# Attention product in three passes, with lists re-ordered, in a two-layer graph kernel

## The reference

```python
# layer 0
q, k = split(X @ Wqk);  v = X @ Wv
agg = einsum('bij,bjd->bid', adj, k * mask)
w = mask * einsum('bid,bid->bi', q, agg) / 16
x = layernorm(x + softmax(w, axis=1)[:, :, None] * v)
# layer 1
query, keyt, value = x @ Wq.T + bq, x @ Wk.T + bk, x @ Wv.T + bv
weight = adj * exp(einsum('bqd,bkd->bqk', query, keyt))
weight = weight / sum(weight, axis=2)
x = layernorm(x + einsum('bqk,bkd->bqd', weight, value))
```

## Time and profile before

| | |
|---|---|
| Median of 3 runs | 305.21 us (304.97 to 305.28) |
| Profiled execution | 305.32 us |
| Its span | 303.5 us |
| TensorE matmul busy | 97% |
| VectorE busy | 75% |
| ScalarE busy | 71% |
| GpSimd busy | 65% |
| Mean granted TensorE clock | 0.994 |
| DMA | 103 GB/s |

### The profile page before, as it was taken

How to read it: one execution, slowest core, us unless ns; L and a number is a source line. 1 busy time by engine, 2 the same in 40 slices (tenths; PEclk the granted TensorE clock), 3 DMA queues, 4 the chain that set the end, 5 groups by cost and what they waited for, 6 DMA issues and landing times.

```text
span 303.5 us, 6829 instructions
## 1 busy us (share of the span) xinstructions
PE 293.9 (97%) x1956; PEld 269.4 (89%) x1956; DVE 227.3 (75%) x691; ACT 215.0 (71%) x509; POOL 198.2 (65%) x237
## 2 busy tenths in 40 slices
PE   8999999999999999999999999999999999999981
PEld 7788999999999999999999999999999999999980
DVE  1476778877777887777788777778877777888583
ACT  3447667778877777887777788777778877776762
POOL 1547766666886666688666667866666787664540
PEclk9999999999999999999999999999999999999997
DMA  7921233332334332224334222434422234210102
GB/s 230 339 73 36 88 89 122 97 107 62 105 121 121 121 113 92 70 89 121 121 121 121 80 73 89 121 121 121 121 89 72 83 119 121 87 54 36 37 35 104
DMA packets 19165, 31.26 MB, mean 103 GB/s; under 512 B 2128, under 2 KB 6608, under 8 KB 19152
## 3 DMA queue, kind: packets, MB, share of 16 engines
q1 hardware_dynamic: 19152, 31.11, 32.6%
HBM read 22.71 MB, written 8.39 MB: 102 GB/s over the span
## 4 chain that ended last, share of the span: by engine, by line
PE 91%; DVE 4%; issue 2%; ACT 1%; POOL 1%; POOLq 0%; DVEq 0%
PE ps L789 22%; PE ps L791 21%; PE ps L790 21%; PE ps L897 8%; PE ps L892 8%; PE ps L874 4%; PE ps L996 1%; PE ps L812 1%; PE ps L849 1%; PE ps L843 1%; DVE stats L571 1%; PE ps L1001 1%; DVE x L609 1%; PE ps L854 1%; POOL x1t_lo_a L303 0%
## 5 line engine op out<-in xcount | busy, mean ns | idle before, releaser
L355 POOL TENSOR_TENSOR rstd<-var_eps,minus_half 128x4 f32<-128x4 f32 x31 | 31.6, 1018 | 72.4 <-DVE var_eps L711 72.4
L431 ACT ACTIVATE x<-x_sum,shift,rstd 128x256 f32<-128x256 f32 x62 | 33.9, 595 | 59.7 <-POOL shift L358 59.6
L789 PE MATMUL ps<-w_hi,xt_hi 128*128 128x512 f32 x128 | 56.8, 444 | 0.5 <-DVE w_lo L775 0.5
L791 PE MATMUL ps<-w_hi,xt_lo 128*128 128x512 f32 x128 | 50.3, 393 | 0.0
L790 PE MATMUL ps<-w_lo,xt_hi 128*128 128x512 f32 x128 | 50.3, 393 | 0.0
L282 POOL TENSOR_TENSOR x1b<-x,bv_all 128x512 f32<-128x512 f32 x32 | 41.3, 1290 | 6.7 <-DVE x L609 3.5
L365 POOL TENSOR_TENSOR xt_lo<-xt_raw,xt_hi 128x512 fp32r<-128x512 f32 x31 | 39.8, 1285 | 3.0 <-ACT xt_hi L413 3.0
L342 POOL TENSOR_TENSOR x_lo<-x_raw,x_hi 128x512 fp32r<-128x512 f32 x28 | 36.1, 1290 | 3.4 <-ACT x_hi L420 2.1
L789 PE MATMUL ps<-wv_hi,x1t_hi 128*128 128x258 f32 x124 | 37.9, 305 | 0.0
L791 PE MATMUL ps<-wv_hi,x1t_lo 128*128 128x258 f32 x124 | 35.3, 285 | 0.0
L790 PE MATMUL ps<-wv_lo,x1t_hi 128*128 128x258 f32 x124 | 35.1, 283 | 0.0
(11 more groups left out here) (128 smaller groups left out, 787.9 us busy)
## 6 DMA issues: line engine op xcount, KB each, us to landing
xt_raw<-xt_pairs SPq DMA_DIRECT2D x32, 256.0 KB, 2.8
x_raw<-x_pairs SPq DMA_DIRECT2D x32, 256.0 KB, 3.1
out_pairs<-x SPq DMA_DIRECT2D x31, 256.0 KB, 2.5
adjt<-adjt_pairs SPq DMA_DIRECT2D x32, 129.0 KB, 2.0
p<-params SPq DMA_DIRECT2D x1, 770.0 KB, 7.1
p<-params SPq DMA_DIRECT2D x1, 512.0 KB, 3.8
p<-params SPq DMA_DIRECT2D x1, 256.0 KB, 4.9
out_pairs<-x SPq DMA_DIRECT2D x2, 128.0 KB, 1.8
```

What stands on the lines that cost most here:

```text
L355: nc.gpsimd.tensor_tensor(rstd[r % 2][:, :, :], var_eps[:, :, :], minus_half[:, :, :], ALU.pow)\
L431: last = nc.scalar.activation(out[:, graph(g)], in_[:, graph(g)], ACT.Identity, bias=shift[r % 2][:, layer, g:g + 1], scale=rstd[r % 2][:, ...
L789: nc.tensor.matmul(out, s_hi, m_hi, start=first, stop=False)
L791: return nc.tensor.matmul(out, s_lo, m_hi, start=False, stop=last)
```

## The change

New tiles `edge_hi`, `edge_lo`, `val_hi`, `val_lo` hold the parts of the edge and of the value, and in the slots the attention product is a `split_product` of these. ScalarE makes edge_hi (a cast) and val_hi (in place of the copy to val), GpSimd makes edge_lo, VectorE makes val_lo from PSUM. In DRAIN and in the drain the product stays as it was.

The lists are re-ordered. TensorE: attend after both halves of project. VectorE: statistics, neg_mean, var_eps and val_lo before x1t_hi and x1t_lo; both weights together before the attention result; statistics of x2 after the maximum of the row. ScalarE: edge_hi after x1t; split_adjm before the z copy. GpSimd: edge_lo first, then rstd and shift, low_x, mask_adj, xt_lo, low_adjm, x1b. In slot 0 the normalization of x1 is done by VectorE, transpose_w stands between the two values, and transpose_p before the transposes of x1. In the drain some steps are cut into halves of the features or into the two graphs and shared between engines.

```diff
@@ GpSimd, drain and slot
-                nc.gpsimd.tensor_tensor(x1t_lo_a[:, :, :, :].rearrange("p t g n -> p (t g n)"),
-                                        x1t_a[:, :, :, :].rearrange("p t g n -> p (t g n)"),
-                                        x1t_hi_a[:, :, :, :].rearrange("p t g n -> p (t g n)").bitcast(F32),
+                nc.gpsimd.tensor_tensor(x1t_lo_a[:, 0, :, :], x1t_a[:, 0, :, :], x1t_hi_a[:, 0, :, :].bitcast(F32),
                                         ALU.subtract).then_inc(x1t_lo_done, 1)
             def slot(t, r):
-                if exists(t + 3) and r + 3 >= SPLIT:
-                    low_x(t + 3, r + 3)
+                if exists(t - 1):
+                    pool.wait_ge(edge_hi_done, t)
+                    nc.gpsimd.tensor_tensor(edge_lo[:, :], edge[:, :], edge_hi[:, :].bitcast(F32), ALU.subtract)\
+                        .then_inc(edge_lo_done, 1)
...
                 if exists(t + 3) and r + 3 >= SPLIT:
+                    low_x(t + 3, r + 3)
                     mask_adj(t + 3, r + 3)
...
+                if exists(t + 3) and r + 3 >= SPLIT:
+                    low_adjm(t + 3, r + 3)
...
-                if exists(t + 3) and r + 3 >= SPLIT:
-                    low_adjm(t + 3, r + 3)
@@ ScalarE, slot
+                if exists(t - 1):
+
+                    act.wait_ge(edge_done, t)
+                    if exists(t - 2):
+                        act.wait_ge(sum_done, t - 1)
+                    nc.scalar.copy(edge_hi[:, :], edge[:, :]).then_inc(edge_hi_done, 1)
...
+                if exists(t + 3) and r + 3 >= SPLIT:
+                    split_adjm(t + 3, r + 3)
                 if exists(t) and r != 0:
                     act.wait_ge(z_done, t + 1)
                     bias_z(z)
...
-                if exists(t + 3) and r + 3 >= SPLIT:
-                    split_adjm(t + 3, r + 3)
...
-                    nc.scalar.copy(val[:, :, 0:DIM], val_ps[:, :, 0:DIM]).then_inc(val_copied, 1)
+                    to = val if r == DRAIN else val_hi
+                    nc.scalar.copy(to[:, :, 0:DIM], val_ps[:, :, 0:DIM]).then_inc(val_copied, 1)
@@ VectorE, slot
-                        dve.wait_ge(sum_done, t - 1)
+                        dve.wait_ge(edge_lo_done, t - 1)
                     nc.vector.tensor_tensor(edge[:, :], exp_s[:, :], adjt[(r - 1) % 4][:, 0:PAIR_N], ALU.mult)\
                         .then_inc(edge_done, 1)
-                if exists(t) and r != 0:
-                    split_x1t(t)
...
+                if exists(t - 1):
+
+                    dve.wait_ge(val_copied, t)
+                    nc.vector.tensor_tensor(val_lo[:, :, 0:DIM], val_ps[:, :, 0:DIM], val_hi[:, :, 0:DIM].bitcast(F32),
+                                            ALU.subtract).then_inc(val_lo_done, 1)
+                if exists(t) and r != 0:
+                    split_x1t(t)
...
-                    weight(t + 2, r + 2, 0)
+                    for g in range(2):
+                        weight(t + 2, r + 2, g)
...
+                if r == 0:
+                    normed_x1(1, 0, norms(0))
+                if exists(t - 1):
+                    dve.wait_ge(x2_done, t)
+                    both_stats(1, x2[(r - 1) % 4]).then_inc(stats2_done, 1)
@@ TensorE, slot
-                if exists(t - 1):
-
-                    pe.wait_ge(edge_done, t)
-                    pe.wait_ge(val_copied, t)
-                    attend(sum_ps, edge, val, 0)
-                    attend(sum_ps, edge, val, 1).then_inc(sum_done, 1)
                 if exists(t + 2):
                     project(t + 2, r + 2, 1)
+                if exists(t - 1):
+
+                    pe.wait_ge(edge_lo_done, t)
+                    pe.wait_ge(val_lo_done, t)
+                    for g in range(2):
+                        n = graph(g, NODES)
+                        mm = split_product(sum_ps[:, g, 0:VAL_COLS], [(edge_hi[:, n], edge_lo[:, n],
+                                                                       val_hi[:, g, :], val_lo[:, g, :])])
+                    mm.then_inc(sum_done, 1)
...
                     values(x1t_hi, x1t_lo, 0)
-                    values(x1t_hi, x1t_lo, 1).then_inc(val_done, 1)
                     if r == 0:
                         transpose_w(2, 2)
+                    values(x1t_hi, x1t_lo, 1).then_inc(val_done, 1)
```

More of the change, by code:

```diff
@@ L96, in build @@
         edge = sb("edge", [128, PAIR_N])
+        edge_hi = sb("edge_hi", [128, PAIR_N], F32R)
+        edge_lo = sb("edge_lo", [128, PAIR_N], F32R)
+        val_hi = sb("val_hi", [128, 2, VAL_COLS], F32R)
+        val_lo = sb("val_lo", [128, 2, VAL_COLS], F32R)
         den_inv = sb("den_inv", [128, 2])
@@ L514, in slot @@
                     bias_z(z)
-                if exists(t + 1):
+                if exists(t + 1) and r != 0:
                     act.wait_ge(shift_done, norms(t))
@@ L612, in attended, with normed_x1 @@
                 last.then_inc(x2_done, 1)
+            def normed_x1(u, r, n):
+                dve.wait_ge(rstd_done, n)
+                for g in range(2):
+                    last = nc.vector.tensor_scalar(x1[u % 2][:, graph(g)], x1_sum[u % 2][:, graph(g)],
+                                                   neg_mean[:, 0, g:g + 1], rstd[r % 2][:, 0, g:g + 1], ALU.add, ALU.mult)
+                last.then_inc(x1_done, 1)
             def bias_scores(u):
@@ L666, in drain @@
                 variance(1)
-                bias_scores(b)
-                weigh_edges(b, edge)
-                dve.wait_ge(sum_done, b + 1)
-                attended(b, sum_ps)
+                dve.wait_ge(val_done, b + 1)
+                nc.vector.tensor_scalar(score_bias[:, :], val_ps[:, :, DIM], s_bias[:, 0:1], None, ALU.add)\
+                    .then_inc(score_bias_done, 1)
+                nc.vector.tensor_copy(val[:, 1, 0:DIM], val_ps[:, 1, 0:DIM]).then_inc(last_val_done, 1)
+                for g in range(2):
+                    n_g = graph(g, NODES)
+                    dve.wait_ge(last_exp_done, g + 1)
+                    nc.vector.tensor_tensor(edge[:, n_g], exp_s[:, n_g], adjt[b % 4][:, n_g], ALU.mult).then_inc(last_edge_done, 1)
+                dve.wait_ge(x1b_done, b + 1)
+                dve.wait_ge(out_stored[b % 4], transfers4(b, b))
+                for g in range(2):
+                    dve.wait_ge(last_sum_done, g + 1)
+                    nc.vector.reciprocal(den_inv[:, g:g + 1], sum_ps[:, g, DIM:DIM + 1]).then_inc(last_den_done, 1)
+                    dve.wait_ge(last_den_done, g + 1)
+                    last = nc.vector.scalar_tensor_tensor(
+                        out=x2[b % 4][:, graph(g)], in0=sum_ps[:, g, 0:DIM], scalar=den_inv[:, g:g + 1],
+                        in1=x1b[b % 2][:, graph(g)], op0=ALU.mult, op1=ALU.add)
+                last.then_inc(x2_done, 1)
                 dve.wait_ge(x2_done, b + 1)
@@ L910, in drain @@
                 pe.wait_ge(x1t_hi_done, a + 1)
-                transpose_x1(x1t_drain_ps, b)
+                pe.wait_ge(z_copied, a + 1)
+                for k in range(HALVES):
+                    for g in range(2):
+                        c = g * DIM + k * 128
+                        half = x1t_ps if k else x1t_drain_ps
+                        mm = nc.tensor.transpose(half[:, k, g, :], x1[b % 2][:, c:c + 128], ident[:, :])
+                mm.then_inc(x1t_done, 1)
                 pe.wait_ge(edge_done, DRAIN + 1)
@@ L927, in drain @@
                 pe.wait_ge(z_copied, b + 1)
-                pe.wait_ge(x1t_copied, b + 1)
+                for k in range(HALVES):
+                    pe.wait_ge(half_copied[k], 1)
                 pe.wait_ge(x2_done, DRAIN + 1)
                 scores(score_ps, z, x1t)
-                pe.wait_ge(edge_done, b + 1)
-                pe.wait_ge(val_copied, b + 1)
-                attend(sum_ps, edge, val, 0)
-                attend(sum_ps, edge, val, 1).then_inc(sum_done, 1)
+                pe.wait_ge(last_val_done, 2)
+                for g in range(2):
+                    pe.wait_ge(last_edge_done, g + 1)
+                    attend(sum_ps, edge, val, g).then_inc(last_sum_done, 1)
             def transpose_next(t, r):
@@ L986, in slot @@
                     scores(score_ps, z, x1t)
[L987 to L990 removed]
+                if r != DRAIN:
                     transpose_p(t + 2, r + 2)
```

75 lines of the change are left out of this document (41 added, 34 removed).

## The result

The kernel after the change takes 307.01 us, median of 4 executions (306.95 to 307.62); the kernel before, measured beside it, took 305.09 (304.83 to 305.28). The ratio is 1.0064, 95% interval 1.0051 to 1.0076: slower by 0.6%. The forecast was 307.7, the fast rival 299.7, rstd's hold 316.7. The profiled execution took 307.62, the longest of the four; its span is 305.8, against 303.5 before. All times are in microseconds (us).

What follows compares the result with a forecast made beforehand. TensorE bounds the loop; the lists feeding it were to make each slot 0.14 us longer. 305.32 + 3.9 (28 slots) - 0.2 (first slot) - 1.35 (drain) = 307.7 us; forecast's range 304.5 to 311, 8-in-10 range 299.3 to 311.

Steps and rivals of the forecast that it cites:

- fast rival: Slot: edge_lo starts 0.2 us later, so neg_mean and var_eps are not held; each slot gains 0.14, 299.7 us; chance 0.2.
- rstd's hold: Slot: rstd on GpSimd keeps VectorE's x1t_hi out until it ends; slot 9.27 us, whole 316.7; chance 0.1.
- The product, 0.87 to 0.73: TensorE's attend product: six three-pass matmuls at 0.121 us replace 0.87 by 0.73, 0.14 less per slot.
- VectorE up to edge_lo: Counting from E, the end of p's transpose: edge ends at E+1.50, edge_lo runs from E+2.01 to E+2.75.
- neg_mean held: VectorE's neg_mean, ready at E+2.16 (E: end of p's transpose), is held by GpSimd's edge_lo and ends at E+2.79.
- From there to the queries: After neg_mean: val_lo from E+2.85 (E: end of p's transpose), x1t_lo done E+4.60, queries wait 0.25; slot 8.92.
- The second chain: GpSimd and ScalarE, from E (p's transpose ended): rstd E+2.94, shift E+4.03, z E+6.80, next p transpose ends E+8.96.
- The sum of the slots: Loop: a slot lasts about 8.95 us, 0.14 more than before; over 28 slots +3.9 us.
- The first slot: Slot 0: x1's normalization leaves ScalarE for VectorE and transposes move; gain between nothing and 0.7 us, taken as -0.2.
- The drain: Whole drain after the loop: -1.35 us, from -0.35 and -1.0, with bounds -0.5 and -2.0.
- The halves of x1t_lo_a: Drain: x1t_lo_a, 1.27 us with TensorE idle 0.45, cut in halves on two engines; at most 0.45, taken as -0.35.
- -1.0 at the end: End of drain, by halves and graphs: 0.2 exponential, 0.2 edge and sum, 0.4 attend, 0.2 copy and queue.

Runs made afterwards that it cites:

- both: Kernel after the change, with val_lo directly behind the edge on VectorE and adjm_hi after the row exponential on ScalarE: 299.34 us, ratio 0.9806.
- quarter_lo: Kernel after the change, order untouched, with edge_lo made for only 64 of its 256 columns: 299.61 us, ratio 0.9819.
- both_olddrain: As both, but with the drain of the kernel before on all engines: 299.48 us, ratio 0.9811.
- best2: both, plus drain x1t_lo_a half from PSUM, slot 0 normalization on ScalarE behind the exponential, drain score_bias and last value copy earlier on VectorE: 298.70 us.
- val_first: Kernel after the change, with only val_lo moved directly behind the edge on VectorE, ahead of the statistics: 305.29 us, ratio 1.0004.
- val_adjm_first: As val_first, and on GpSimd the masked adjacency placed ahead of the low part of x: 299.05 us, ratio 0.9794.

## Why the prediction was right, point by point

- *The product, 0.87 to 0.73.* Right: 0.74. In both, where nothing else waits, a slot is 0.20 shorter than before (8.824 to 8.624), 0.06 more than the product explains. Taken from the chain in time, as means over 16 slots before and 22 in both, the product is 0.145 shorter, the values 0.03 (1.46 to 1.43) and the queries 0.02 (1.43 to 1.41); the projection is the same (2.79). Why the matmuls of the values and queries are some 0.002 shorter each stays open.
- *VectorE up to edge_lo.* Right to 0.01: edge ends at E+1.50, edge_lo starts at E+2.02 (2.01) and ends at E+2.76 (2.75).
- *neg_mean held.* Right: predicted to end at E+2.79, ended at E+2.78. This was the step on which everything hung, and one neg_mean in the drain beside an x1b was enough to see it. quarter_lo and both show that it is the cause of the loss.
- *From there to the queries.* 0.09 too long: val_lo started at E+2.77, not E+2.85, because var_eps started 0.08 before neg_mean ended, as it does when nothing is held. x1t_lo was done at E+4.51 instead of 4.60, and the wait was 0.17 instead of 0.25.
- *The second chain.* rstd at E+2.94 and shift at E+4.03 as predicted; from the held shift on again 0.08 too long (x_lo at E+4.52 for 4.60; z at E+6.73 for 6.80). It ends at the scores, which wait for z; I had it go on to p_row and the transpose of p. p_row starts at 161.13 and takes 0.34, the scores end at 161.79, so p_row was ready 0.3 ahead of TensorE.
- *The sum of the slots.* The mechanism was right and the size off: +0.085 per slot instead of +0.14, and 28 times the difference is the 1.5 us. Two parts make it up. In 23 of the 28 slots the step is 0.095 (8.806 before, 8.901 after), since both chains end earlier than I had them. The other five, some 0.1 longer before (8.906), take 8.944 after, so that they pay only 0.04. I had the loop's branch cost as before. If these five are the slots with the branch, as their number and their distance of four slots in the kernel before suggest, some 0.06 of its 0.10 no longer shows.
- *The first slot.* The sign was wrong. I priced only what ScalarE was rid of and not how the normalization would fare on VectorE: beside xt_lo of GpSimd it takes 1.58 where the one in the drain took 0.74, and p_row waits behind it. Timelines of VectorE and GpSimd of the kernel after:

```profile
25.83 1.58 DVE L641 TENSOR_SCALAR x<-x_sum,neg_mean,rstd 128x256 f32<-128x256 f32 x2
...
25.66 1.28 POOL L374 TENSOR_TENSOR xt_lo<-xt_raw,xt_hi 128x512 fp32r<-128x512 f32 x1
```

  From x1t_hi of slot 0 to p_col of slot 1 that is 7.24 instead of 7.11, +0.13. The other 0.22 of the start lies ahead of slot 0, and 0.20 of it ahead of the first copy of p_col, which stands at 14.98 here and at 14.78 before. Over the twelve kernels with the new lists, which compute the same up to there, that copy stands anywhere from 14.32 to 15.00. So this part isn't the change's.
- *The drain.* The term was mis-sized, -1.35 for -0.42 (0.37 in the comparison of both and both_olddrain), below my lower bound of 0.5. Two steps failed. The halves of x1t_lo_a were to save 0.35, but the two engines stood in each other's way: GpSimd's half took 0.97 while VectorE's ran, and TensorE's idle time fell from 0.45 to 0.15. And -1.0 at the end was worked out from the idle times of TensorE and VectorE at the last product, with no look at VectorE's list ahead of it. That list is full (timeline of VectorE, kernel after):

```profile
296.51 0.70 DVE L595 BATCH_NORM_STATS2 stats<-x 128x6 f32<-128x512 f32 x1
...
297.40 0.21 DVE L703 TENSOR_SCALAR score_bias<-ps,s_bias 128x2 f32<-128x2 f32 x1
...
298.32 0.55 DVE L709 TENSOR_TENSOR edge<-exp_s,adjt 128x128 f32<-128x128 f32 x2 [0.38 <-ACT exp_s L495]
299.56 0.17 DVE L714 RECIPROCAL den_inv<-ps 128x1 f32<-128x1 f32 x1 [0.69 <-PE ps L951]
```

  The halves do shorten the waits (0.69 for the last product, where the earlier trace rows has 1.23), but the exponentials can't start before score_bias, and that stands behind the statistics of pair 30's output, which the end doesn't wait for. best2 moved it and got 0.25.
- *The fast rival.* It needed a start of edge_lo near E+2.2; it came at E+2.02. But its price was about right: in val_first, both and val_adjm_first, where neg_mean slips past, x1t_lo ends at E+4.07, and both, which frees the second chain too, is at 299.34 against its 299.7. That closeness is in part luck: in both the slots gave 5.6 where the rival had 4.1 (it also counts 29 slots, the sum 28), and the ends gave 0.4 where it had 1.55. quarter_lo shows that freeing neg_mean alone is enough; val_first shows that it isn't when it is bought by putting val_lo ahead of the statistics.
- *rstd's hold.* Refuted. rstd ran from 155.96 to 156.98, and x1t_hi from 156.39 to 156.80 took 0.41 beside it, as in the earlier trace rows. The Trainium skill ("SBUF — State Buffer", Who interferes with whom) says that the one that starts first "gets the shared pair for the whole instruction": for edge_lo over neg_mean, x1t_lo over shift and xt_lo over the normalization the traces agree (0.62, 0.54 and 1.58 instead of 0.17, 0.20 and 0.74); for rstd they don't.

## What to carry to other kernels

When an instruction is put on GpSimd, look at what VectorE starts while it runs: a 0.17 us instruction of four elements that begins 0.14 after a 0.74 us one costs the rest of it, and everything queued behind pays. The repair is order. Here val_lo went ahead, so that the statistics, which edge_lo doesn't hold (0.71 beside it), lay in that stretch and neg_mean came just behind it. Then follow the other chain through the same edit, since what is moved ahead on one list is moved ahead of that chain's first link too. And where two chains end within 0.1 us of each other, single edits show almost nothing (2.0 and 1.7 us here), and the pair shows 7.7; a change that "did not help" may be half of one that does.

## What the runs showed of the hardware that I had not expected

- rstd, a power of 128x4 on GpSimd, lasts 1.02 us and lets VectorE's cast and subtraction run at full speed beside it: x1t_hi takes 0.41 inside it in the kernel after, and x1t_lo 0.69 inside it in val_first. The subtractions of 128x256 and 128x512 on GpSimd held neg_mean, the edge and the normalization to their end, but not the statistics (0.71 beside edge_lo in val_first). Started while x1t_hi ran on VectorE, rstd took 1.12 (val_first); had it been held until x1t_hi ended, 0.25 after its start, it would have come to 1.27.
- val_lo, a subtraction with one input in PSUM and one in SBUF, takes 0.68 for 128x512, the same as x1t_lo with both in SBUF (0.69); in the drain, where VectorE's half of x1t_lo_a read one input from PSUM instead of SBUF, what that saved was the hold: GpSimd's half beside it took 0.73 instead of 0.97.
